# Attention and feed-forward in one pass: the products run thirteen chunks behind the attention instead of fourteen, and two row tiles share a chunk

## Chip, cores and metric

The kernel runs on one core of a Trainium2 chip. The metric is the device time of one execution in microseconds, the median of several runs. TensorE is called PE in the profile, VectorE DVE, ScalarE ACT, GpSimd POOL, and SyncE (which here only issues DMAs) SP.

## What is computed

The inputs are `x` and `ctx`, each 8 batches of 512 positions by 2048 channels.

```python
# attention by autocorrelation, d = 256 channels a head, H = 8 heads
q, k = layernorm(x), ctx                       # v = ctx as well
corr = ifft(fft(q) * conj(fft(k))).real        # along the 512 positions, each channel
w, idx = top_k(corr, 12); w = softmax(w)       # 12 lags for each channel
out = sum_i w[i] * v[min(idx[i] + pos, 511)]   # shifted values, the last one repeated
x1 = x + out
# feed-forward: one 2048 x 2048 matrix plus 16 low-rank updates, weighted
h = layernorm(x1)
y = h @ W.T + bias + sum_e coeffs[e]*scales[e] * (h @ A[e].T) @ Bf[e].T
result = x1 + y
```

## The kernel before, in words

The attention works on chunks of one batch and 256 channels: 8 chunks a batch, 64 in all. Transforms are matrix products with cosine and sine matrices on folded halves of the positions. The feed-forward folds its low-rank updates into W first, splits W and h into high and low float16 halves, and takes three of the four products of halves. A batch's feed-forward needs all 8 of its attention chunks.

**Windows.** Every engine runs one loop over windows `w`. In window `w` the attention handles chunk `w` (queries, correlation, the largest lags, weights) and the output of chunk `w - 1`. PE begins window `w` with the lag products of chunk `w - 1` (`upper_lags`, L756), and in this document a window begins there, or with its first feed-forward product when no attention is left. The feed-forward of batch `b` takes 8 windows, `8b + LAG` to `8b + LAG + 7`, in which `fill` (L878) slips 8 pieces of 12 matmuls (L848, L850, L852) between the steps of the attention. With LAG = 14 windows 0 to 13 hold attention alone, 14 to 63 both, 64 to 77 products (window 64 also has the lag products and the output of the last chunk). In windows 1 to 9 the engines also prepare W.

**Row tiles.** Between the two halves a batch passes through 4 row tiles of 128 positions by 2048 channels. Tile `r` goes this way, one tile a window in windows `8b + 9` to `8b + 12`:

- SP loads the tile of x into `rows[w % 2]`, one of two buffers (`load_rows`, L497).
- POOL issues a DMA that adds the attention's parts onto it (`add_row`, L1211).
- DVE takes its statistics (`row_statistics`, L1445 to L1450), does the attention's `part_output` (L1438, L1439), and then the inverse root and shift (`row_gain`, up to L1458).
- SP stores the tile as x1 to the output (`store_x1`, L513). When that has landed ACT normalises it (L1051) and copies the high half (L932); POOL subtracts for the low half (`row_low`, L1217) in the next window.
- SP stores both halves (`store_h`, L517 and L519). When all four tiles of a batch have landed, `load_h` (L549) turns and loads them for PE.

**Output.** Every second product window ends a group of 512 output columns. At the start of the window after it DVE multiplies the sums out of PSUM into `y`, one of two buffers (`scale_group`, L1467; L1286 in the profile), and POOL adds them onto the output with a DMA (L1238). PE may not start the next group on a PSUM bank before DVE has read it (the wait in L846).

Every engine takes its instructions in program order, and SP and POOL wait in line for the semaphore of each DMA that they issue. The attention's chain on POOL within a window is `add_products`, `add_upper`, `add_lower` (which ends in `z_added`), after which PE may run `output` (L828).

## Time and profile before

| | us |
|---|---|
| median of 3 runs (2583.07 to 2590.03) | 2583.85 |
| the profiled execution's own time | 2574.18 |
| its span, first to last instruction | 2572.4 |
| PE busy | 2438.0 (95%) |
| DVE busy | 1798.4 (70%) |
| POOL busy | 1785.6 (69%) |
| ACT busy | 1103.5 (43%) |

The profile is of one execution. It is read by stretches, since the stages have different limits: the front, windows 0 to 13, up to 496.59 us; the shared windows up to about 2250 us; the end with products alone. A wait is told with what ended it. A bracket at the end of a row gives the engine's idle time ahead of the instruction, and its releaser.

### The profile page before, as it was taken

To read this page: it belongs to the slowest core of one execution; us is meant where nothing else is said; L and a number is where in the kernel's file an instruction comes from. 1 tells how busy PE (TensorE), PEld (TensorE's weight loads), DVE (VectorE), ACT (ScalarE), POOL (GpSimd) and SP (SyncE) were. 2 spreads that over 40 slices of the span, in tenths; PEclk is the share of its full clock that TensorE was granted. 3 is DMA by queue.
4 is the path that set the end of the run, shared out by engine and by line. 5 is a ranking of instruction groups with operands and counts; after the bars stand their busy time and mean duration, and the time that the engine had idled before them with its cause. 6 is when DMAs were issued, how large, how long until landed. Compare 5 with 4: busy or idle time off the path is not lost.

```text
span 2572.4 us, 36321 instructions
## 1 busy us (share of the span) xinstructions
PE 2438.0 (95%) x12536; PEld 1529.4 (59%) x12536; DVE 1798.4 (70%) x4366; ACT 1103.5 (43%) x2166; POOL 1785.6 (69%) x1357
## 2 busy tenths in 40 slices
PE   4998966799999999999999999999999999999898
PEld 3665655566666666666666666666666666644343
DVE  5888887767887688777876788768877787731000
ACT  4787865543454344543454344444433343201000
POOL 5798988866986688876886788677886688422000
PEclk8999998899999999999999999999999999999999
DMA  9499999966999789968998799968996799689853
GB/s 336 101 262 263 273 227 243 266 200 192 285 293 237 203 245 290 262 186 246 288 281 197 196 303 291 254 174 243 284 247 172 212 294 245 134 244 311 220 138 86
DMA packets 532264, 606.03 MB, mean 236 GB/s; under 512 B 322160, under 2 KB 447216, under 8 KB 509168
## 3 DMA queue, kind: packets, MB, share of 16 engines
q1 hardware_dynamic: 505920, 503.04, 66.4%
q0 software_dynamic: 26160, 100.67, 20.2%
q8 instruction: 99, 1.62, 0.2%
q14 instruction: 85, 0.70, 0.1%
HBM read 342.53 MB, written 184.56 MB: 205 GB/s over the span
## 4 chain that ended last, share of the span: by engine, by line
PE 77%; issue 4%; DMA 3%; POOL 3%; SPq 2%; DVE 1%; ACT 0%; POOLq 0%; ACTq 0%; DVEq 0%
PE f_ps L848 16%; PE f_ps L850 16%; PE f_ps L852 16%; PE a_ps L699 10%; PE a_ps L756 5%; PE a_ps L829 3%; PE a_ps L828 3%; PE a_ps L761 2%; PE a_ps L801 2%; DMA p_lo_t<-p_lo 1%; PE a_ps L807 1%; PE a_ps L809 1%; PE a_ps L803 1%; DMA out_dram<-a_rows 1%; PE f_ps L874 1%
## 5 line engine op out<-in xcount | busy, mean ns | idle before, releaser
L848 PE MATMUL f_ps<-f_whi,f_hhi 128*128 128x512 f16 x2048 | 777.8, 380 | 15.2 <-issue 7.5
L850 PE MATMUL f_ps<-f_wlo,f_hhi 128*128 128x512 f16 x2048 | 777.7, 380 | 0.0
L852 PE MATMUL f_ps<-f_whi,f_hlo 128*128 128x512 f16 x2048 | 777.5, 380 | 0.0
L1140 POOL TENSOR_TENSOR a_zvf<-a_zvf,a_twf 128x512 f32<-128x512 f32 x256 | 337.2, 1591 | 79.3 <-DVE a_twf L1286 79.3
L852 PEld LDWEIGHTS f_ps<-f_whi,f_hlo 128*128 128x128 f16 x2048 | 200.7, 98 | 242.6 <-issue 1.9
L1140 POOL TENSOR_TENSOR a_prod<-a_prod,a_twf 128x512 f32<-128x512 f32 x64 | 81.6, 1274 | 368.5 <-DVE a_twf L1286 321.6
L848 PEld LDWEIGHTS f_ps<-f_whi,f_hhi 128*128 128x128 f16 x2048 | 200.8, 98 | 229.2 <-issue 15.3
L850 PEld LDWEIGHTS f_ps<-f_wlo,f_hhi 128*128 128x128 f16 x2048 | 200.7, 98 | 225.5 <-issue 1.4
L932 ACT ACTIVATE a_vu<-a_ps 128x512 f32<-128x512 f32 (+2 forms) x512 | 218.2, 486 | 157.4 <-PE a_ps L699 156.7
L756 PE MATMUL a_ps<-a_w_lag,lags 128*128 128x256 f16 x1536 | 231.5, 274 | 11.0 <-DVE a_twf L1286 10.4
L1286 DVE TENSOR_TENSOR a_twf<-a_ps,a_vu 128x1024 f32<-128x1024 f32 (+1 forms) x128 | 223.5, 1746 | 0.2 <-PE a_ps L699 0.2
L1286 DVE TENSOR_TENSOR f_y<-f_ps,f_scale 128x512 f32<-128x512 f32 x128 | 80.0, 682 | 198.4 <-PE f_ps L852 198.4
L932 ACT ACTIVATE a_side<-a_ps 128x1 f32<-128x1 f32 (+2 forms) x420 | 122.5, 333 | 183.4 <-PE a_ps L829 168.7
L1286 DVE TENSOR_TENSOR a_zvf<-a_ps,a_vu 128x2048 f32<-128x2048 f32 x64 | 146.5, 2290 | 55.7 <-PE a_ps L756 55.7
L756 PEld LDWEIGHTS a_ps<-a_w_lag,lags 128*128 128x128 f16 x1536 | 150.3, 98 | 54.0 <-DVE a_twf L1286 12.6
L1140 POOL TENSOR_TENSOR a_zu<-a_zu,a_zvf 128x512 f32<-128x512 f32 x128 | 179.4, 1579 | 0.0
L1140 POOL TENSOR_TENSOR a_zu<-a_zu,a_tu 128x512 f32<-128x512 f32 x128 | 165.6, 1358 | 19.2 <-DVE a_tu L1286 19.2
L1217 POOL TENSOR_TENSOR f_rowlo<-a_rows,f_rowhi 128x2048 f16<-128x2048 f32 x32 | 136.4, 4262 | 41.1 <-ACT f_rowhi L932 41.1
L1051 ACT ACTIVATE a_rows<-a_rows,f_shift,f_gain 128x2048 f32<-128x2048 f32 x32 | 67.1, 2095 | 208.1 <-DVE f_shift L1458 134.2
L1024 ACT ACTIVATE a_prod<-a_ps,a_minus_max 128x512 f32<-128x512 f32 x128 | 81.0, 684 | 165.5 <-issue 158.9
L942 ACT ACTIVATE xs<-xs,stat 128x256 f32<-128x256 f32 x256 | 132.2, 589 | 35.1 <-DVE stat L1429 31.7
L1238 POOL DMA_DIRECT2D out_dram<-f_y x31 | 48.3, 1558 | 139.4 <-DVE f_y L1286 130.1
(145 smaller groups left out, 5047.6 us busy)
## 6 DMA issues: line engine op xcount, KB each, us to landing
f_whi<-whi_scratch SPq DMA_DIRECT2D x128, 512.0 KB, 5.2
f_wlo<-wlo_scratch SPq DMA_DIRECT2D x128, 512.0 KB, 6.0
a_rows<-in_x_dram SPq DMA_DIRECT2D x62, 1024.0 KB, 9.8
vs<-in_ctx_dram SPq DMA_DIRECT2D x64, 512.0 KB, 6.2
xs<-in_x_dram SPq DMA_DIRECT2D x64, 512.0 KB, 6.0
parts_scratch<-a_so SPq DMA_DIRECT2D x64, 512.0 KB, 7.3
a_rows<-parts_scratch POOLq DMA_DIRECT2D x32, 1024.0 KB, 10.2
out_dram<-a_rows SPq DMA_DIRECT2D x32, 1024.0 KB, 11.4
```

The lines of the kernel that those rows point to most:

```text
L699: return nc.tensor.matmul(ps[:, pair, j, :], fold[:, k, :], source, start=True, stop=True)
L756: mm = nc.tensor.matmul(out, lag_mat[:, constant, 2 * cls + k, :], w_lag[:, part, main::TB, :], start=(constant + part == 0), stop=(consta ...
L828: nc.tensor.matmul(ps[:, 2 + j, i, :], outm[:, k0, :], z[:, s0, :], start=True, stop=False)
L848: nc.tensor.matmul(f_ps[:, t, :], h_hi[q][:, kq, rows_t], w_hi[u % WR][:, :, kq, :], start=(k == 0), stop=False)
L850: nc.tensor.matmul(f_ps[:, t, :], h_hi[q][:, kq, rows_t], w_lo[u % WR][:, :, kq, :], start=False, stop=False)
L852: mm = nc.tensor.matmul(f_ps[:, t, :], h_lo[q][:, kq, rows_t], w_hi[u % WR][:, :, kq, :], start=False, stop=(k == DB - 1))
L932: return nc.scalar.activation(out, source, ACT.Copy, **how)
L942: op = nc.scalar.activation(xs[n % XB][:, k, :], xs[n % XB][:, k, :], ACT.Identity, bias=gain[:, 1, k:k + 1], scale=gain[:, 0, k:k + 1])
L1024: nc.scalar.activation(wts[:, g, :], corr[:, g, :], ACT.Exp, bias=minus_max[:, g:g + 1]).then_inc(exp_done, 1)
L1140: return nc.gpsimd.tensor_tensor(whole, whole, part, op)
L1217: nc.gpsimd.tensor_tensor(row_lo[:, :], rows[w % 2][:, :], row_hi[:, :], ALU.subtract).then_inc(lo_done, 1)
L1286: return nc.vector.tensor_tensor(out, a, b, ALU.mult)
```

## The change

LAG goes from 14 to 13. For that the four row tiles of a batch are done in three windows: tile 0 in window `8b + 9`, tiles 1 and 2 in `8b + 10`, tile 3 in `8b + 11`. The buffer of a tile now goes by the tile's parity and not by the window's. The high and low halves get two buffers each, and the semaphores of the stores of x1 and of the halves are split by parity to go with them. The space comes from `y`, which has one buffer now, so that DVE may write a group only when the DMA of the group before has landed. The closing of a batch's statistics for the attention moves from window 13 to window 12 of its batch.

```diff
-LAG, KQ, WR = 14, 4, 3
+LAG, KQ, WR = 13, 4, 3
...
-        row_hi = sb("f_rowhi", [T, D], F16)
-        row_lo = sb("f_rowlo", [T, D], F16)
+        row_hi = [sb(f"f_rowhi{i}", [T, D], F16) for i in range(2)]
+        row_lo = [sb(f"f_rowlo{i}", [T, D], F16) for i in range(2)]
...
-        y = [sb(f"f_y{i}", [T, TB, WC]) for i in range(2)]
+        y = sb("f_y", [T, TB, WC])
...
+        def row_window(r):
+
+            return CHUNKS * (r // TB) + 9 + (0, 1, 1, 2)[r % TB]
+
+        def row_tiles(w):
+
+            return [r for r in range(TILES) if row_window(r) == w]
...
+            def load_row(r):
+
+                w, i = row_window(r), (r + 1) % 2
+                before = stats_before(w, i)[-1]
+                at_least(sp, rows_done, sum(stats_tile(k) is not None for k in range(before + 1)))
+                at_least(sp, lo_done, r - 1)
+                at_least(sp, pw_summed, 2 * min(w - 2, PREPARED))
+                sp.dma_start(rows[i][:, :], x_rows[r * T:(r + 1) * T, :]).then_inc(rows_in[i], 16)
...
-                if row_tile(w - 1) is not None:
-                    store_h(row_tile(w - 1))
+                for r in row_tiles(w - 1):
+                    store_h(r)
+                    if r % TB < 2:
+                        load_row(r + 2)
...
-                if r is not None:
-                    store_x1(w, r)
+                for r in row_tiles(w):
+                    if r % TB < 2:
+                        store_x1(r)
...
                 load_v(w + 3)
+                for r in row_tiles(w):
+                    if r % TB >= 2:
+                        store_x1(r)
...
-                if r is not None and r % TB > 0:
-                    add_row(w, r)
-                if row_tile(w - 1) is not None:
-                    row_low(w - 1, row_tile(w - 1))
+                for r in row_tiles(w):
+                    if r % TB == 1:
+                        add_row(r)
+                for r in row_tiles(w - 1):
+                    row_low(r)
                 if 1 <= w <= N:
                     add_upper(w - 1)
...
                 if 1 <= w <= N:
                     add_lower(w - 1)
+                for r in row_tiles(w):
+                    if r % TB >= 2 or r % TB == 0 and w < LAG:
+                        add_row(r)
...
-                at_least(dve, out_out[g % 2], 16 * (g // 2))
+                at_least(dve, out_out, 16 * g)
...
-                if r is not None:
-                    row_statistics(w, r)
+                first = [r for r in row_tiles(w) if r % TB < 2]
+                for r in first:
+                    row_statistics(r)
                 if 1 <= w <= N:
                     part_output(w - 1)
-                if r is not None:
+                for r in first:
+                    row_gain(r)
+                for r in row_tiles(w)[len(first):]:
+                    row_statistics(r)
                     row_gain(r)
```

DVE, batch 3, from the end of tile 1's root to the attention's next products (`a_prod`): before.

```order
L153 TENSOR_SCALAR f_gain<-f_sq,f_root 128x1
L1458 TENSOR_SCALAR f_shift<-f_mv,f_gain 128x1
L1286 TENSOR_TENSOR a_prod<-a_ps,a_vu 128x1024
L1286 TENSOR_TENSOR a_twf<-a_ps,a_vu 128x1024
L1286 TENSOR_TENSOR a_zu<-a_ps,a_vu 128x1024
```

The same place after the change, up to the first step of tile 2's root.

```order
L153 TENSOR_SCALAR f_gain<-f_sq,f_root 128x1
L1491 TENSOR_SCALAR f_shift<-f_mv,f_gain 128x1
L1478 BN_STATS f_bn<-a_rows 128x6 x4
L116 MEMSET a_idle 1x1
L1481 BN_AGGR f_mv<-f_bn 128x2
L1483 TENSOR_SCALAR f_veps<-f_mv 128x1
L142 TENSOR_SCALAR f_root<-f_veps 128x1
```

Tile 2's statistics and root now stand ahead of `a_prod`, and after them the four `f_y` products of `scale_group`, which before stood one window earlier and one later.

POOL, the window after tile 1's (window 35 of batch 3), from the attention's `add_products` to `z_added`: before.

```order
L1140 TENSOR_TENSOR a_prod<-a_prod,a_twf 128x512
L1184 TENSOR_TENSOR a_prod<-a_twf,a_prod 128x512
L1211 DMA a_rows<-parts_scratch 128x2048
L1217 TENSOR_TENSOR f_rowlo<-a_rows,f_rowhi 128x2048
L1140 TENSOR_TENSOR a_zu<-a_zu,a_tu 128x512 x2
L1223 DMA out_dram<-f_bias 128x2048
L1140 TENSOR_TENSOR a_zvf<-a_zvf,a_twf 128x512 x4
L1140 TENSOR_TENSOR a_zu<-a_zu,a_zvf 128x512 x2
```

The same window after the change.

```order
L1166 TENSOR_TENSOR a_prod<-a_prod,a_twf 128x512
L1210 TENSOR_TENSOR a_prod<-a_twf,a_prod 128x512
L1244 TENSOR_TENSOR f_rowlo<-a_rows,f_rowhi 128x2048 x2
L1166 TENSOR_TENSOR a_zu<-a_zu,a_tu 128x512 x2
L1251 DMA out_dram<-f_bias 128x2048 x2
L1266 DMA out_dram<-f_y 128x4x512
L1166 TENSOR_TENSOR a_zvf<-a_zvf,a_twf 128x512 x4
L1166 TENSOR_TENSOR a_zu<-a_zu,a_zvf 128x512 x2
L1238 DMA a_rows<-parts_scratch 128x2048
```

Two subtractions for low halves stand ahead of the attention's sums, and tile 3's accumulate comes behind them.

SP, last batch, from tile 0's stores of its halves (tiles 28 to 31 of the program): before.

```order
L517 DMA h_scratch<-f_rowhi 128x2048
L519 DMA h_scratch<-f_rowlo 128x2048
L497 DMA a_rows<-in_x_dram 128x2048
L513 DMA out_dram<-a_rows 128x2048
L538 DMA f_whi<-whi_scratch 128x2048
L538 DMA f_wlo<-wlo_scratch 128x2048
```

The same place after the change.

```order
L532 DMA h_scratch<-f_rowhi 128x2048
L534 DMA h_scratch<-f_rowlo 128x2048
L512 DMA a_rows<-in_x_dram 128x2048
L528 DMA out_dram<-a_rows 128x2048
L553 DMA f_whi<-whi_scratch 128x2048
L553 DMA f_wlo<-wlo_scratch 128x2048
L528 DMA out_dram<-a_rows 128x2048
L553 DMA f_whi<-whi_scratch 128x2048
L553 DMA f_wlo<-wlo_scratch 128x2048
L577 DMA f_scale<-wscale_scratch 128x512
L532 DMA h_scratch<-f_rowhi 128x2048
L534 DMA h_scratch<-f_rowlo 128x2048
```

Tile 2's store of x1 (the second L528) now stands ahead of the next weights, of the load of the scales, and of tile 1's halves, which the load of tile 3 comes behind; before it stood behind all of these.

## Rows read from the trace of the kernel before

**Rows 1.** The page, part 1: busy time of each engine.

```profile
PE 2438.0 (95%) x12536; PEld 1529.4 (59%) x12536; DVE 1798.4 (70%) x4366; ACT 1103.5 (43%) x2166; POOL 1785.6 (69%) x1357
```

**Rows 2.** Stretches: length, busy us (instructions) by engine, clock, DMA share, GB/s.

```profile
366.09:397.31 31.22, 21.98 (x114) 17.40 (x113) 26.67 (x67) 17.24 (x30) 30.41 (x21) 0.89 1.09 224
431.40:465.44 34.04, 22.11 (x114) 17.51 (x113) 26.67 (x67) 16.98 (x30) 27.91 (x22) 0.90 1.05 266
465.44:496.59 31.15, 21.74 (x105) 16.82 (x104) 24.19 (x54) 21.07 (x35) 29.08 (x23) 0.84 1.06 254
496.59:535.70 39.11, 36.93 (x189) 22.78 (x188) 26.34 (x68) 17.84 (x39) 24.12 (x20) 0.96 0.94 231
1202.17:1237.25 35.08, 35.08 (x189) 22.42 (x188) 29.31 (x75) 15.59 (x33) 30.66 (x23) 1.00 1.06 291
2277.70:2298.43 20.73, 20.73 (x98) 9.39 (x97) 6.00 (x20) 0.79 (x1) 1.79 (x2) 1.00 0.83 230
2395.01:2417.77 22.76, 22.76 (x97) 9.91 (x98) 0.00 (x0) 0.00 (x0) 0.00 (x0) 0.91 1.11 254
```

**Rows 3.** DVE in order of time, around window 34: start, length, instruction.

```profile
1200.36 2.47 DVE L1286 TENSOR_TENSOR f_y<-f_ps,f_scale 128x512 f32<-128x512 f32 x4
1202.75 1.21 DVE L1286 TENSOR_TENSOR a_prod<-a_ps,a_vu 128x1024 f32<-128x1024 f32 x1
...
1228.80 2.46 DVE L1445 BATCH_NORM_STATS2 f_bn<-a_rows 128x6 f32<-128x512 f32 x4
...
1231.67 0.69 DVE L1438 TENSOR_TENSOR a_so<-a_ps,a_side 128x512 f32<-128x512 f32 x1
...
1235.30 0.21 DVE L1458 TENSOR_SCALAR f_shift<-f_mv,f_gain 128x1 f32<-128x1 f32 x1
```

**Rows 4.** PE in order of time, window 34: second lag products, output.

```profile
1206.51 0.49 PE L756 MATMUL a_ps<-a_w_lag,lags 128*128 128x256 f16 x3
...
1226.89 0.59 PE L828 MATMUL a_ps<-a_zu,outm 128*128 128x256 f32 x2
```

**Rows 5.** POOL in order of time, window 34, from `add_products` to `z_added`.

```profile
1205.17 1.28 POOL L1140 TENSOR_TENSOR a_prod<-a_prod,a_twf 128x512 f32<-128x512 f32 x1 [9.08 <-DMA parts_scratch<-a_so]
...
1208.24 4.39 POOL L1217 TENSOR_TENSOR f_rowlo<-a_rows,f_rowhi 128x2048 f16<-128x2048 f32 x1
1212.28 2.78 POOL L1140 TENSOR_TENSOR a_zu<-a_zu,a_tu 128x512 f32<-128x512 f32 x2
...
1221.01 3.65 POOL L1140 TENSOR_TENSOR a_zu<-a_zu,a_zvf 128x512 f32<-128x512 f32 x2
```

**Rows 6.** DMA issues, 1206 to 1227 us (window 34): the last number is us to landing.

```profile
a_rows<-parts_scratch POOLq DMA_DIRECT2D x1, 1024.0 KB, 9.5
a_rows<-in_x_dram SPq DMA_DIRECT2D x1, 1024.0 KB, 10.1
```

**Rows 7.** The same, 1241 to 1250 us (window 35).

```profile
a_rows<-parts_scratch POOLq DMA_DIRECT2D x1, 1024.0 KB, 11.9
a_rows<-in_x_dram SPq DMA_DIRECT2D x1, 1024.0 KB, 16.1
```

**Rows 8.** SP in order of time, window 35 (begun at 1237.25): the load of a tile.

```profile
1247.06 0.37 SPq L497 DMA_DIRECT2D a_rows<-in_x_dram  x1
```

**Rows 9.** SP and DVE in order of time, batch 0's window 10 (366.09 to 397.31).

```profile
389.88 0.34 SPq L497 DMA_DIRECT2D a_rows<-in_x_dram  x1
...
397.90 1.22 DVE L1286 TENSOR_TENSOR a_prod<-a_ps,a_vu 128x1024 f32<-128x1024 f32 x1
```

**Rows 10.** SP, DVE and PE in order of time, the end.

```profile
2332.67 0.37 SPq L497 DMA_DIRECT2D a_rows<-in_x_dram  x1
...
2336.52 2.47 DVE L1445 BATCH_NORM_STATS2 f_bn<-a_rows 128x6 f32<-128x512 f32 x4 [24.81 <-DMA a_rows<-parts_scratch]
...
2342.90 0.38 PE L848 MATMUL f_ps<-f_whi,f_hhi 128*128 128x512 f16 x1 [2.84 <-DVE f_y L1286]
```

More of the change, by code:

```diff
@@ L426, in closed_batch, with stats_before, rows_job @@
                 return 1
-            return (w - 13) // CHUNKS + 2 if w >= 13 and (w - 13) % CHUNKS == 0 and (w - 13) // CHUNKS < BATCH - 2 else None
-        def rows_job(w):
-            return sum(stats_tile(i) is not None or row_tile(i) is not None for i in range(w % 2, w + 1, 2))
-        def row_tile(w):
-            if w >= 9 and (w - 9) % CHUNKS < 4 and (w - 9) // CHUNKS < BATCH:
-                return TB * ((w - 9) // CHUNKS) + (w - 9) % CHUNKS
-            return None
+            return (w - 12) // CHUNKS + 2 if w >= 12 and (w - 12) % CHUNKS == 0 and (w - 12) // CHUNKS < BATCH - 2 else None
+        def row_window(r):
+            return CHUNKS * (r // TB) + 9 + (0, 1, 1, 2)[r % TB]
+        def row_tiles(w):
+            return [r for r in range(TILES) if row_window(r) == w]
+        def stats_before(w, parity):
+            return [i for i in range(w) if i % 2 == parity and stats_tile(i) is not None]
+        def rows_job(w, parity):
+            return len(stats_before(w + 1, parity)) + sum(row_window(r) <= w and (r + 1) % 2 == parity for r in range(TILES))
         def product_window(w):
@@ L486, in load_v, with load_stats @@
                 shared.load_v(sp, n)
-            def load_rows(w):
-                m, r = stats_tile(w), row_tile(w)
-                if m is None and r is None:
+            def load_stats(w):
+                m = stats_tile(w)
+                if m is None:
                     return
                 at_least(sp, rows_done, sum(stats_tile(i) is not None for i in range(w - 1)))
-                at_least(sp, lo_done, sum(row_tile(i) is not None for i in range(w - 1)))
+                at_least(sp, lo_done, max([r + 1 for r in range(TILES) if (r + 1) % 2 == w % 2 and row_window(r) < w],
+                                          default=0))
                 at_least(sp, pw_summed, 2 * min(w - 2, PREPARED))
-                source = r if m is None else m + TB
-                sp.dma_start(rows[w % 2][:, :], x_rows[source * T:(source + 1) * T, :]).then_inc(rows_in[w % 2], 16)
+                sp.dma_start(rows[w % 2][:, :], x_rows[(m + TB) * T:(m + TB + 1) * T, :]).then_inc(rows_in[w % 2], 16)
+            def load_row(r):
[5 more added lines that the diff above has]
+                sp.dma_start(rows[i][:, :], x_rows[r * T:(r + 1) * T, :]).then_inc(rows_in[i], 16)
             def store_parts(n):
@@ L630, in _ @@
                 if 0 < w <= PREPARED:
-                    load_rows(w + 1)
+                    load_stats(w + 1)
+                    for r in row_tiles(w + 1):
+                        load_row(r)
                 load_x(w + 3)
@@ L1045, in copy_output, with row_normalise, row_high @@
                 copy(skew[:, :, :], ps[:, 2:4, 1, :]).then_inc(out_copied, 1)
-            def row_normalise(w, r):
+            def row_normalise(r):
+                row = rows[(r + 1) % 2]
                 act.wait_ge(f_shift_done, r + 1)
-                act.wait_ge(x1_out, 16 * (r + 1))
-                nc.scalar.activation(rows[w % 2][:, :], rows[w % 2][:, :], ACT.Identity, bias=f_shift[:, 0:1],
-                                     scale=f_gain[:, 0:1]).then_inc(h_done, 1)
-            def row_high(w, r):
+                act.wait_ge(x1_out[r % 2], 16 * (r // 2 + 1))
+                nc.scalar.activation(row[:, :], row[:, :], ACT.Identity, bias=f_shift[:, 0:1], scale=f_gain[:, 0:1]
+                                     ).then_inc(h_done, 1)
+            def row_high(r):
                 act.wait_ge(h_done, r + 1)
-                at_least(act, h_out, 32 * r)
-                copy(row_hi[:, :], rows[w % 2][:, :]).then_inc(hi_done, 1)
+                at_least(act, h_out[r % 2], 32 * (r // 2))
+                copy(row_hi[r % 2][:, :], rows[(r + 1) % 2][:, :]).then_inc(hi_done, 1)
             def tile_sums(w, n):
@@ L1273, in _ @@
                     add_lower(w - 1)
+                for r in row_tiles(w):
+                    if r % TB >= 2 or r % TB == 0 and w < LAG:
+                        add_row(r)
                 if w == PREPARED + 2:
```

93 lines of the change are left out of this document (48 added, 45 removed).

## The prediction, made before the changed kernel ran

> **What bounds the kernel now.** I read the busy times first: PE is busy 95% of the span, the next engine 70% [rows 1]. That average hides three stages, so I cut the span at the windows [rows 2]. Window 34, in the shared stage, takes 35.08 us with PE busy all of it: the bound is PE alone. A window with attention alone takes 31 to 34 us with PE busy 22: there the bound is the chain through POOL, DVE and ACT, with the DMA engines full (share above 1). A window with products alone takes 20.73 us. Next come the instructions around window 34, for how much time each engine has in hand before PE must wait [rows 3 to 8], and last the front [rows 9] and the end [rows 10].
>
> What the smaller LAG is worth: one attention window becomes shared, one window of products alone goes. Windows 13 and 14 took 31.15 + 39.11 us (the 39.11 holds the wait for the first products); as two shared windows they take 39.11 + 35.08, so +3.9. The window that goes was worth 20.7, but the end of the kernel must be able to use it. From the start of window 65 (2277.70) to the first product of the last batch (2395.01) there were 117.3 us, and PE's own work in them was 5 x 20.7 = 103.6. The rest was waiting for the row tiles.
>
> **The shared stage: batches 1 to 6, six double windows.** I take window 34 (start 1202.17) with tiles 1 and 2 of its batch, and write +x for us after a window's start.
>
> DVE. Tile 1's statistics start at 1228.80, +26.6, and its shift ends at 1235.51, +33.3, the attention's two outputs (1.2) among them. A tile alone is 2.87 (1228.80 to 1231.67) plus 6.71 - 2.87 - 1.2 = 2.6, so 5.5 [rows 3]. Tile 2 behind it ends at +38.8, 3.8 into window 35. By the new parity the four `f_y` stand next, 2.4 (1200.36 to 1202.75), then the attention's two products, 2.4: done at +8.5 of window 35. PE wants them before its second lag products at +4.34 (1206.51 - 1202.17) [rows 4]. In window 35 PE waits 4.2, part of it already on the first product of the new group, which needs `f_y`.
>
> POOL. It starts `add_products` when DVE's products are done, at +8.5 in place of +3.0, and needed 19.5 to the end of `z_added` (1205.17 to 1224.66) [rows 5]. Now two low halves stand in that stretch: 4.04 more (1208.24 to 1212.28). The issue of a second bias DMA comes in and the issue of an accumulate goes out, which cancels. So `z_added` is at 8.5 + 19.5 + 4.0 = +32.1, where PE wanted to start the output at +24.7 (1226.89) [rows 4]. PE's whole wait in window 35 is 7.4, DVE's 4.2 inside it.
>
> Tile 2's data. Its load is issued where tile 3's was, at about +9.8 [rows 8], lands 10.1 [rows 6] or 16.1 [rows 7] later, POOL issues the accumulate right behind (it is there at about +20), and that lands 9.5 or 11.9 later: +29.4 to +37.8. DVE wants it at +33.3. So 0 to 4.5 more; I take 1.8, a little below the middle, since the group's DMA has left window 34.
>
> Tile 3. POOL issues its accumulate behind `z_added`, at +32.1 of window 35; it lands at +41.6 to +44. DVE's 5.5 follow, and 2.4 of products: +49.5 to +51.9. Window 36 starts at 35.08 + 7.4 = 42.5 and wants the products 4.34 later, at +46.8: 2.7 to 5.1 of wait. I take 3.0. Behind DVE in line stand the attention's next chunk, and behind POOL's accumulate the folds for the next chunks; they have a window in hand.
>
> Sum: 7.4 + 1.8 + 3.0 = 12.2 a batch, 73 for six. Nothing gives it back, since PE had no idle time in these windows. Bounds: 4.2 (DVE alone counts) to 7.4 + 4.5 + 5.1 = 17, so 25 to 102.
>
> The Trainium skill ("DMA: Bandwidth & Descriptors", Issuing engines are not separate DMA queues) says that DMAs started by SP and by GpSimd run on the same 16 engines and only interleave. By that rule two tiles in one window find no second path, and each should land like the slower row; by that the 1.8 would be 4.5, and the total 16 more. The trace agrees so far as the same load took 10.1 in one window and 16.1 in the next [rows 6, 7].
>
> **The front (batch 0).** Tile 2's load goes out at 389.88 [rows 9], lands about 10 later at 400, the accumulate (up to 11.9 here) at about 412, and DVE needs 5.5: 417.4, where the attention's next products began at 397.90 [rows 9]. That is 19.5, with POOL's folds held up behind the accumulate too. Tile 3 does the like one window on; from the shared stage I take 5. Window 12 loses its tile, and a window without the stall of one is 3 shorter (34.04 against 31.15) [rows 2]. 19.5 + 5 - 3 = 21.5. Bounds 5 (the landings are hidden) and 30.
>
> **The end.** In window 66 DVE now waits for tile 2's accumulate, which landed at 2336.5 [rows 10], 58.8 after window 65 began; its load still hangs on tile 0. `f_y` of the group finished in window 66 stands behind that and 5.5 of statistics, so PE begins window 67 at about +65, and is through window 68 at 65 + 2 x 20.7 = +106, +108.5 if it restarts as slowly as window 70 did (22.76 against 20.73) [rows 2]. Before, the same wait stood a window later and cost 2.84 [rows 10]. SP also holds tile 1's halves and tile 3's load behind tile 2's store and the load of the scales: the load goes out at about +65.5, where it was at +55.0 (2332.67) [rows 10]. If everything from that load to the first product takes its old 62.3 us, the last batch starts at +127.8. With fewer weights loaded meanwhile it will be less. Between 108.5 and 127.8 I take 118, which is +1 to the 117.3. The window saved is not seen here. Bounds: -34 (PE alone, 4 x 20.7 = 83) and +11.
>
> **Sum.** 3.9 + 73 + 21.5 + 1 = +99. The one buffer of `y` costs nothing in it: a group's DMA has two windows, 70 us, to land. On the profiled execution: its span 2572.4, its own time 2574.18, so 2673 us. The median of the runs shown lies 9.7 above that execution, so I give 2583.85 + 99 = 2683.
>
> **Rivals.**
> - It fits, and the end shortens (faster). DVE is only 29.3 of 35.08 busy in window 34 [rows 2], room for 5.5 by the sum. If the shared and front windows hold their time and the last batch starts when PE is free, 3.9 - 34.4 = -30: 2553. Against it: the room lies ahead of +26.6, where DVE waits in its chain, and the last tile's path runs through four landings one after another. 0.07.
> - The two cancel: 25 + 3.9 + 5 - 34: 2584. It needs the end at PE's limit, against the 58.8 us of tile 2. 0.04.
> - DVE's overflow alone: POOL's low halves find room. 25 + 3.9 + 5 to 12: 2618 to 2625. Against it, the 19.5 that I read. 0.11.
> - The clock. In the windows where PE waits, the granted clock drops from 2.4 to 1.2 GHz for a while, as ahead of window 70 (clock 0.91, 2.0 us lost) [rows 2]. Twelve such windows at 2.0: +24, 2707. Against it: these waits are shorter than the 13.7 us of waiting ahead of window 70, and lie between full stretches. 0.15.
>
> The Trainium skill ("TensorE: Matmul & The Clock Gate", Why this matters for your kernels) warns that idle gaps between bursts of matmuls send the clock back to half rate. By it the clock is likelier to drop on the longer waits than on those of 2 to 4 us. The row of window 70 agrees for the waits ahead of it.
>
> **How the numbers follow.** My own case has 0.63. All but the first two rivals are slower. Range: low 2630 (7.4 x 6 = 44, LAG 3.9, front 5, end -8), high 2725 (six at 16 is 96, 3.9, 30, 11); what lies below and above is 2 in 10. A measurement tells about 0.3%, 8 us, from no change: faster 0.07, same 0.04, slower 0.89.
>
> **What would show it.** Right: in the window after each double one PE waits on `f_y` and on the lag products' release, then at L828's output for POOL's `a_zu`, some 7 us together; that window is about 42.5 us and the one behind it 38; twelve longer windows and the rest at 35.08. In the front DVE waits for the accumulate in window 10. In the end PE stands some 23 us ahead of window 67. Wrong: those windows at 35.08, or the last batch starting 83 to 100 us after window 65. I am most in doubt about tile 3 and the last chain.

## The result, and the profile of the changed kernel

The changed kernel takes 2752.26 us, the median of 4 runs (2744.47 to 2764.84); the kernel before, beside it, 2583.46 (4 runs, 2576.97 to 2590.03). The ratio is 1.0658, 95% interval 1.063 to 1.0686: slower. The direction had been forecast, the size not: +99 us forecast, +169 measured. The profiled execution took 2744.47, its span is 2742.7, so 170.3 more than the span of before.

Busy times on the page of the changed kernel:

```profile
PE 2469.0 (90%) x12516; PEld 1536.9 (56%) x12516; DVE 1821.9 (66%) x4372; ACT 1098.2 (40%) x2168; POOL 1789.3 (65%) x1359
```

PE does the same matmuls as in [rows 1] (some records are missing) and is busy 31.0 us longer for them. Next the stretches, as in [rows 2] (length, busy us of PE, PEld, DVE, ACT and POOL, granted clock, DMA share, GB/s): windows 9, 11, 12, then 34, 35, 36, then from window 65 to the last batch's first product, and the window behind it.

```profile
330.62:374.05 43.43, 21.48 (x114) 16.77 (x112) 27.77 (x72) 20.35 (x34) 28.58 (x20) 0.79 0.93 201
405.59:459.05 53.46, 24.06 (x113) 19.02 (x112) 27.41 (x69) 21.21 (x32) 44.98 (x31) 0.71 0.96 233
459.05:501.47 42.42, 22.34 (x105) 17.52 (x104) 28.78 (x71) 18.29 (x34) 28.94 (x23) 0.80 0.88 223
1282.77:1317.85 35.08, 35.08 (x190) 22.43 (x189) 29.37 (x76) 15.47 (x33) 29.80 (x23) 1.00 1.02 276
1317.85:1366.91 49.06, 35.81 (x190) 22.11 (x188) 30.11 (x77) 17.78 (x34) 36.05 (x26) 0.99 1.03 259
1366.91:1406.79 39.88, 38.15 (x189) 23.38 (x189) 33.25 (x83) 17.05 (x36) 28.44 (x21) 0.93 0.95 262
2433.52:2563.42 129.90, 86.04 (x386) 38.10 (x384) 26.36 (x82) 16.01 (x8) 27.15 (x15) 0.83 0.91 248
2563.42:2586.03 22.61, 22.61 (x97) 9.83 (x98) 0.00 (x0) 0.00 (x0) 0.00 (x0) 0.91 1.09 284
```

Against before, whose windows 9, 11 and 12 took 35.28, 34.09 and 34.04, the 170.3 split as follows. "A window like 35" is the one at that place in its batch: 19, 27, 35, 43, 51 and 59.

- Windows 9 to 12: +36.2.
- Windows 13 and 14, where LAG acts: +4.3.
- Windows 15 to 64: +115.5, 113.5 of it in three windows a batch: those like 35 average 48.8 (47.6 to 51.4), like 36 39.3, like 37 36.1. The others stay within about 1 us of 35.08.
- The end: +12.6 (129.9 against 117.3), and behind it +1.9, the last window.

Window 35 on PE, only the rows with a wait (start, length, instruction, in brackets the wait ahead of it and what ended it):

```profile
1322.39 0.38 PE L874 MATMUL f_ps<-f_whi,f_hhi 128*128 128x512 f16 x1 [2.64 <-DVE f_y L1319]
...
1326.36 0.50 PE L782 MATMUL a_ps<-a_w_lag,lags 128*128 128x256 f16 x3 [1.22 <-DVE a_twf L1319]
...
1349.96 0.67 PE L854 MATMUL a_ps<-a_zu,outm 128*128 128x256 f32 x2 [3.05 <-POOL a_zu L1166]
...
1366.91 0.82 PE L782 MATMUL a_ps<-a_w_lag,lags 128*128 128x256 f16 x3 [6.34 <-DMA a_w_lag<-a_w_row]
```

The first three sum to 6.9, where 7.4 was forecast. The last is new: window 36 cannot begin, since the transposed lag weights have not landed. SP turns these weights with two transposing DMAs, called the lag transposes below, and in the shared stage every window begins with the products that use them. Here is SP's row of their issue:

```profile
1348.01 14.00 SPq L523 DMA_TRANSPOSE a_w_lag<-a_w_row  x2
```

The DMAs issued from 1338 to 1350 (last number: median us to landing):

```profile
out_dram<-f_bias POOLq DMA_DIRECT2D x2, 1024.0 KB, 11.0
out_dram<-f_y POOLq DMA_DIRECT2D x1, 1024.0 KB, 20.2
a_rows<-parts_scratch POOLq DMA_DIRECT2D x1, 1024.0 KB, 16.9
a_w_lag<-a_w_row SPq DMA_TRANSPOSE x2, 17.4
```

In the kernel before, window 34, where a group's DMA was still in flight, had for the same pair:

```profile
a_w_lag<-a_w_row SPq DMA_TRANSPOSE x2, 6.1
```

and windows 32 and 40, with nothing of GpSimd's in flight, 3.1 and 3.2 us. SP is held by the issue too, for 14 us, with weights, the store of x1 and the parts behind it. On DVE and ACT tile 3 is then late in window 36:

```profile
1365.53 2.47 DVE L1478 BATCH_NORM_STATS2 f_bn<-a_rows 128x6 f32<-128x512 f32 x4 [9.92 <-DMA a_rows<-parts_scratch]
```

```profile
1375.46 2.09 ACT L1078 ACTIVATE a_rows<-a_rows,f_shift,f_gain 128x2048 f32<-128x2048 f32 x1 [21.17 <-DMA out_dram<-a_rows]
```

PE's rows of all six batches add the 113.5 us up, to within rounding: 37.0 are waits for DVE and POOL inside the windows like 35 (the three rows above), 31.4 are waits for the lag transposes at their end (3.5 to 6.9 each), 7.4 are waits for the next lag transposes at the end of the windows like 36, 5.7 are other short waits in windows like 36 and 37, and 32.2 are busy time that PE has more for the same products. Some 26 of the 32.2 are the clock, an estimate: in 13 stretches of windows 15 to 63, 61.4 us in all, it was granted at its lower level (1.2 GHz), PE was busy for 51.9 us of them, and half of that is lost.

### The profile page after: what moved, and what is told of

The parts are those of the page before. It is cut to its first block and busy times, and to the rows that moved or that the text cites. A ratio compares the mean times of both kernels' runs of the same rounds, so it can differ in the third digit from the quotient of the medians.

```text
span 2742.7 us, 36295 instructions
## 1 busy us (share of the span) xinstructions
PE 2469.0 (90%) x12516; PEld 1536.9 (56%) x12516; DVE 1821.9 (66%) x4372; ACT 1098.2 (40%) x2168; POOL 1789.3 (65%) x1359
## 5 line engine op out<-in xcount | busy, mean ns | idle before, releaser
L1166 POOL TENSOR_TENSOR a_zvf<-a_zvf,a_twf 128x512 f32<-128x512 f32 x256 | 330.0, 1478 | 92.7 <-DVE a_twf L1319 92.7
L782 PE MATMUL a_ps<-a_w_lag,lags 128*128 128x256 f16 x1536 | 243.2, 284 | 84.6 <-DVE a_twf L1319 43.7
L782 PEld LDWEIGHTS a_ps<-a_w_lag,lags 128*128 128x128 f16 x1536 | 153.3, 101 | 137.9 <-DVE a_twf L1319 51.4
L1078 ACT ACTIVATE a_rows<-a_rows,f_shift,f_gain 128x2048 f32<-128x2048 f32 x32 | 67.1, 2096 | 351.3 <-DMA out_dram<-a_rows 221.9
L958 ACT ACTIVATE a_side<-a_ps 128x512 f32<-128x512 f32 (+1 forms) x422 | 122.2, 330 | 202.5 <-PE a_ps L855 185.4
L1478 DVE BATCH_NORM_STATS2 f_bn<-a_rows 128x6 f32<-128x512 f32 x128 | 78.9, 680 | 163.2 <-DMA a_rows<-parts_scratch 163.2
L1166 POOL TENSOR_TENSOR a_zu<-a_zu,a_tu 128x512 f32<-128x512 f32 x128 | 162.2, 1305 | 19.5 <-DVE a_tu L1319 19.5
L1166 POOL TENSOR_TENSOR a_zu<-a_zu,a_zvf 128x512 f32<-128x512 f32 x128 | 172.3, 1469 | 0.0
L958 ACT ACTIVATE a_tu<-last 1x256 f32<-1x256 f32 x64 | 26.2, 410 | 321.4 <-DVE a_tu L1319 321.4
```

The source lines that it names most:

```text
L782: mm = nc.tensor.matmul(out, lag_mat[:, constant, 2 * cls + k, :], w_lag[:, part, main::TB, :], start=(constant + part == 0), stop=(consta ...
L958: return nc.scalar.activation(out, source, ACT.Copy, **how)
L1078: nc.scalar.activation(row[:, :], row[:, :], ACT.Identity, bias=f_shift[:, 0:1], scale=f_gain[:, 0:1]).then_inc(h_done, 1)
L1166: return nc.gpsimd.tensor_tensor(whole, whole, part, op)
L1478: op = nc.vector.bn_stats(f_bn[:, j, :], rows[(r + 1) % 2][:, j * WC:(j + 1) * WC])
```

## Experiments

First the change was taken apart from its far end. Each kernel of this ladder differs from the next by one group of edits; all times are medians, the ratio is to the kernel before, timed on the same chip. The last columns are from the traces: windows 9 to 14, 15 to 64, and window 65 to the last batch's first product. A trace is of one execution, and two of these lie well off their median: that of e2 took 15.5 less, that of e1 13.9 more. So a step of the last columns need not equal the step of the medians.

```
kernel                                     us       ratio (95%)              9-14   15-64    end
before                                     2583.5   1                        204.9  1742.1   117.3
own halves, one y, DVE's order (g2)        2597.9   1.0062 (1.0033, 1.0091)  219.3  1749.6   117.7
+ closing, scales a window earlier (g1)    2638.3   1.0217 (1.0184, 1.0250)  225.9  1784.8   117.4
+ SP stores x1 of tiles 2, 3 later (f1)    2661.1   1.0303 (1.0270, 1.0335)  233.4  1784.6   129.0
+ POOL's later accumulates (e2)            2704.9   1.0465 (1.0429, 1.0500)  230.1  1803.5   143.5
+ tiles 1 and 2 share a window (e1)        2783.8   1.0764 (1.0729, 1.0800)  239.7  1900.3   142.6
+ LAG 13: the changed kernel               2752.3   1.0658 (1.0630, 1.0686)  245.4  1857.5   129.9
```

**Single tiles, LAG 14 (e2).**

```
-LAG, KQ, WR = 13, 4, 3
+LAG, KQ, WR = 14, 4, 3
-            return CHUNKS * (r // TB) + 9 + (0, 1, 1, 2)[r % TB]
+            return CHUNKS * (r // TB) + 9 + (0, 1, 2, 3)[r % TB]
```

> The changed kernel with LAG 14 and one row tile a window again, at windows 9, 10, 11, 12. What is left of the change: own halves for even and odd tiles, one y, the places of the later tiles' accumulates and of tile 0's in batch 0, the statistics' closing one window earlier. My theory says that these cost next to nothing but in batch 0 (tile 0's accumulate moved behind the lower sums: window 9 is 8 longer than before): 2592, with window 34 to 36 at 35.08. Rival (the later place of the accumulates of tiles 2 and 3 costs in each batch, 2 to 3 us each): 2610 to 2620.

2704.88 us. Both theories fell short: with no shared window and the old LAG 122 us stay. Windows 36 and 37, and the end:

```profile
1326.95:1364.51 37.56, 35.65 (x189) 22.18 (x188) 27.98 (x66) 15.23 (x32) 29.85 (x23) 1.00 0.95 260
1364.51:1406.79 42.28, 37.71 (x188) 23.41 (x189) 31.95 (x90) 21.25 (x41) 29.36 (x22) 0.92 0.97 266
2363.86:2507.32 143.46, 105.39 (x482) 47.05 (x481) 27.99 (x84) 16.02 (x8) 27.22 (x15) 0.88 0.89 240
```

At the end tile 31's x landed at 2425.14, but POOL issues the accumulate behind tile 30's low half:

```profile
2447.78 4.06 POOL L1244 TENSOR_TENSOR f_rowlo<-a_rows,f_rowhi 128x2048 f16<-128x2048 f32 x1 [27.43 <-ACT f_rowhi L958]
2451.79 0.86 POOL L1251 DMA_DIRECT2D out_dram<-f_bias  x1
2452.39 1.59 POOL L1266 DMA_DIRECT2D out_dram<-f_y  x1
2453.14 1.78 POOL L1238 DMA_DIRECT2D a_rows<-parts_scratch  x1
```

**The same, POOL's accumulates in their old places (f1).**

```
                 for r in row_tiles(w):
-                    if r % TB == 1:
+                    if r % TB > 0:
                         add_row(r)
...
-                    if r % TB == 0 and w >= LAG:
+                    if r % TB == 0:
...
-                for r in row_tiles(w):
-                    if r % TB >= 2 or r % TB == 0 and w < LAG:
-                        add_row(r)
```

> The kernel with single tiles and LAG 14 (1.0465 of before), and in it alone the accumulates on POOL back where they were before the change: tiles 1 to 3 right behind the attention's products, tile 0 ahead of the bias. New theory (POOL's late place of the accumulates is what cost the 120 us there: 59 in the shared windows, 25 in the front, 26 at the end, where tile 31's accumulate went out 28 us after its data had landed): all of it goes, 2590, with the windows at 35.08 and the last batch 117 us after window 65. Rival (own halves, one y or SP's later store of x1 carry part of it): 2620 to 2660; the one y would show as DVE waiting for the group's DMA, the store of x1 as ACT waiting for it.

2661.08: 44 of the 122 go, not all. The two traces differ by 29.9 only, 14.5 of it at the end and 19 in the shared windows. The rival named a part of the rest rightly: tile 3's accumulate landed at 1337.9, SP stored its x1 16.7 us later, behind the lag transposes, and ACT waited:

```profile
1354.52 0.74 SPq L528 DMA_DIRECT2D out_dram<-a_rows  x1
```

```profile
1362.84 2.09 ACT L1078 ACTIVATE a_rows<-a_rows,f_shift,f_gain 128x2048 f32<-128x2048 f32 x1 [12.84 <-DMA out_dram<-a_rows]
```

**And SP's stores of x1 in their old place (g1).**

```
                 for r in row_tiles(w):
-                    if r % TB < 2:
-                        store_x1(r)
+                    store_x1(r)
...
-                for r in row_tiles(w):
-                    if r % TB >= 2:
-                        store_x1(r)
```

> The kernel with single tiles, LAG 14 and POOL's old places (1.0303 of before), and in it SP's stores of x1 back where they were, ahead of the lag transposes. Theory (in the profiled run tile 3's accumulate landed at 1337.9 and its x1 store went out at 1354.5, so ACT stood 12.8 us for it and everything behind it in window 37 was late): ACT's wait goes, window 37 from some 40 to 36, the end 129 to 119, in the front 10 us: 2661 - 6 x 4 - 10 - 10 = 2617. Rival (the closing of the statistics one window earlier, 3.0 us on DVE ahead of window 37's products, makes window 37): only the end and the front gain, 2640.

2638.26, 23 less: the rival's total. The end gave 11.6 back (129.0 to 117.4), and window 37 went from 40.7 to 36.8 as the theory had it, but windows 22, 30 and 38 are 4.5 to 9.2 longer than 35.08 in this kernel, so windows 15 to 64 sum to the same. Windows 9, 36, 37 and the end:

```profile
333.52:376.39 42.87, 22.82 (x113) 18.12 (x112) 25.70 (x68) 17.98 (x32) 25.12 (x19) 0.79 0.95 198
1323.33:1359.55 36.22, 35.25 (x190) 22.33 (x188) 30.47 (x77) 15.59 (x32) 30.42 (x23) 1.00 1.04 274
1359.55:1396.34 36.79, 35.25 (x189) 22.37 (x188) 29.29 (x78) 21.48 (x41) 28.66 (x22) 1.00 0.98 256
2344.09:2461.49 117.40, 105.78 (x481) 47.19 (x480) 28.01 (x84) 16.01 (x8) 27.12 (x15) 0.97 1.01 288
```

**And the closing of the statistics and the stores of the scales in their old windows (g2).**

```
-            return (w - 12) // CHUNKS + 2 if w >= 12 and (w - 12) % CHUNKS == 0 and (w - 12) // CHUNKS < BATCH - 2 else None
+            return (w - 13) // CHUNKS + 2 if w >= 13 and (w - 13) % CHUNKS == 0 and (w - 13) // CHUNKS < BATCH - 2 else None
...
-                if PREPARED <= w < PREPARED + TB:
-                    for n in range(TB * (w - PREPARED), TB * (w - PREPARED + 1)):
+                if PREPARED + 1 <= w < PREPARED + 1 + TB:
+                    for n in range(TB * (w - PREPARED - 1), TB * (w - PREPARED)):
```

> As the kernel before it, and the closing of the statistics and the stores of the weights' scales back in their old windows. What is left of the change: own halves for even and odd tiles, one y, the later tiles' statistics behind the attention's output on DVE, the places of x loads. Theory (those cost nothing): 2580 to 2590, window 9 at 35 again (the scale stores stood ahead of the store of the parts, for which tile 0's accumulate waits). Rival (one y or own halves cost): above 2600, with DVE waiting for the group's DMA.

2597.87, 40 less. Windows 9, 36 and the end:

```profile
329.96:363.64 33.68, 20.95 (x114) 16.71 (x113) 26.18 (x69) 19.15 (x33) 24.87 (x18) 0.90 0.97 264
...
1288.30:1324.77 36.47, 35.42 (x190) 22.28 (x188) 30.68 (x78) 15.59 (x32) 30.64 (x23) 1.00 1.05 271
2298.77:2416.49 117.72, 105.96 (x482) 47.14 (x481) 28.00 (x84) 16.01 (x8) 27.12 (x15) 0.97 1.01 287
```

Window 9 gives 9.2 back, which settles it: the scale stores stood ahead of the store of the attention's parts, for which tile 0's accumulate waits. The parts land 5.0 us after their issue here, 10.4 in the changed kernel, and POOL issues the accumulate 0.6 behind the landing in both. Windows like 37 give 1.7 each back (the closing is some 3 us of DVE ahead of the next products). Windows 22, 30 and 38 are at 35.08 again; in g1 PE waited there for lag transposes (9.1 us ahead of window 23). SP issued them at +34.5, +34.2 and +30.6 of the window, where +26.0 is usual, and they took 8.9 to 9.8 us with nothing of GpSimd's in flight. Why was not settled. What is left, 16 us, a little above the theory, was not taken apart further. In the traces it lies in the windows like 36 (1.1 to 1.9 each, 7.9 in all, where PE waits 0.96 for DVE's products, and the later tiles' statistics now stand behind the attention's output on DVE) and in the front, 14.4. The front's windows scatter: f3 below, with the front of the kernel before, has 210.2 in place of 204.9. No wait of DVE for a group's DMA shows.

**Shared window, LAG 14 (e1).**

```
-LAG, KQ, WR = 13, 4, 3
+LAG, KQ, WR = 14, 4, 3
```

> The changed kernel with LAG back at 14; the shared window of two row tiles, own halves and one y stay. The groups finish in even windows again, so no f_y stands ahead of the attention's products in window 35 and no group's DMA in it. My theory (the group's DMA stretches the lag transposes): window 35 is 40 us, with 1.8 of wait for DVE inside 4.9 for POOL, and the transposes land in 3 to 7 us; window 36 is 37 to 38. Sum against before: 6 x (5 + 2.5) + 8 for the front, and the end 5 to 14 shorter, since tile 31 comes a window earlier ahead of an unmoved window 70: 2625. Rival (tile 3's accumulate stretches the transposes): they still take 15 to 18 us, window 35 is 45 to 46, the time 2655.

2783.8, well above both. Windows like 34 take 41.2 now and windows like 35 50.1. The groups finish in even windows again, so their DMA stands in GpSimd's queue ahead of tile 2's accumulate, and the first lag transpose of the windows like 34 lands in 13.5 to 15.4 us; in those like 35 in 11 to 26 beside tile 3's accumulate, with no group's DMA there. So both theories had a piece: whatever of GpSimd's is in flight counts. By the medians LAG 13 gains 1% against this kernel.

**What holds the lag transposes.** Five kernels, all from the changed one; only the added lines are shown. In e3 the group's DMA is cut to 16 of 128 partitions, which leaves seven eighths of that group out of the output. In e4 tile 3's accumulate is cut the same way:

```
+                part = T // 8 if g % 4 == 2 else T
+                nc.gpsimd.dma_start(out[b, :, cols].rearrange("(i p) d -> p i d", p=T)[0:part], y[0:part, :, :],
```

```
+                part = T // 8 if r % TB == 3 and r >= TB else T
+                nc.gpsimd.dma_start(rows[i][0:part, :], part_rows[r * T:r * T + part, :], accum_op=ALU.add
```

> The changed kernel, with the group's DMA to out in windows 19, 27, 35 and so on (the third group of a batch) cut to 16 of 128 partitions, so seven eighths of that group's products are left out of the output. My theory (that DMA stretches the lag transposes behind it): in window 35 the transposes land in 3 to 8 us in place of 17.9, the wait of 6.3 before the upper lags goes to under 1, and window 35 is 42 to 43 in place of 49.1; time 2752 - 7 x 6 = 2710. Rival (tile 3's accumulate does it): transposes stay at 15 to 18, window 35 at 48 to 49.

> The changed kernel, with the accumulate of the attention's parts onto tile 3 of batches 1 to 7 cut to 16 of 128 partitions (the other rows of that tile lack the attention's output). My theory (the group's DMA stretches the transposes, tile 3's accumulate only adds to it): transposes at 12 to 16 us, window 35 at 46 to 48; window 36, which waits for DVE behind this accumulate, 2 to 3 shorter than its 39.9. Rival (tile 3's accumulate stretches them): transposes in 3 to 8, window 35 at 42 to 43.

Tile 3's accumulate behind the transposes (f4), as a plain load, which leaves x out of that tile (f5), and ahead of the group's DMA (f6, where it is then skipped at its old place):

```
+                        if r % TB == 3 and LAG <= w < N:
+                            pool.wait_ge(w_dma, 32 * dma_turns(w + 1))
                         add_row(r)
```

```
+                how = {} if r % TB == 3 and r >= TB else dict(accum_op=ALU.add)
```

```
                 for r in row_tiles(w - 1):
                     add_bias(r)
+                for r in row_tiles(w):
+                    if r % TB == 3 and LAG <= w < N:
+                        add_row(r)
                 if g is not None:
                     add_group(g)
```

> The changed kernel, with POOL waiting for the lag transposes to land before it issues tile 3's accumulate (batches 1 to 6). The time at which that accumulate landed (47.6 into window 35) is about where it would land anyway from an issue at 37 to 38. Theory (an accumulate of the parts and the lag transposes in flight together hold each other up): the transposes land in 6.5 to 11 us (the group's DMA stays beside them), the last wait of window 35 goes from 6.3 to under 1.5, and window 35 from 49 to 43; window 36 stays within 1.5 of 39.9. Time 2752 - 6 x 6 = 2716. Rival (bias and group DMAs do it, or the number of DMAs in flight): transposes stay at 15 to 18.

> The changed kernel, with tile 3's accumulate (batches 1 to 7) as a plain load of the same bytes from the same queue, without the addition (that tile then holds the attention's output without x). If the addition is what holds the transposes up: they land in 6 to 11 us, window 35 at 43. If it is any DMA of GpSimd's queue, or its place behind the group's DMA in that queue: 15 to 18, window 35 at 48 to 49. I lean to the second, 0.6.

> The changed kernel, with tile 3's accumulate (batches 1 to 6) on POOL ahead of the group's DMA and of the attention's lower sums, at about +23 of window 35, where its load has just landed (in the profiled run 1340.85, POOL comes by at 1340.5). Theory (overlap with the transposes, and the late place): it lands at +34 to +36, only 4 us into the transposes, which take 6 to 11; window 35 43 to 44; DVE has tile 3 in time, so window 36 36 to 37 in place of 39.9. Time 2752 - 6 x 9 = 2698. Rival (transposes wait for whatever GpSimd's queue holds when they are issued, now the group's DMA behind the accumulate, landing at +44): transposes at 15, window 35 at 46 to 48, only window 36 gains, 2725.

Window 35 of each, in us from the issue of the first transpose; "mean" is over the six windows of that place:

```
                       group's DMA  accumulate  transposes    mean 35  mean 36   time us
changed kernel            12.7         17.5     17.9, 18.8      48.8     39.3    2752.3
small group's DMA (e3)     9.4         31.6     31.5, 32.6      50.3     39.7    2749.4
small accumulate (e4)     12.0         13.4     13.9, 14.7      44.7     39.3    2716.5
accumulate later (f4)     11.7          -       12.2, 13.1      43.9     49.8    2774.2
plain load (f5)           12.1         14.7     15.1, 16.0      45.9     39.7    2729.1
accumulate first (f6)     15.5          9.6     16.0, 16.9      47.6     39.5    2745.4
before, window 34          5.6          -        6.5,  7.4
before, window 32           -           -        3.2,  4.4
```

In every row with a DMA of GpSimd's the second transpose lands 1 to 2 us behind the last of them that was issued before it, whether it adds or only loads, large or small. The traces of all 18 kernels say the same of every window: where such a DMA, issued before the second transpose, landed over 8 us after the issue of the first (88 pairs), the second transpose landed 0.2 to 1.9 us behind it. It is not the only thing that counts: of 678 pairs with none in flight half took 4.4 to 4.5 us, but some up to 9.8. Whether the transposes wait their turn or share the same engines no run tells.

The row of e3 is its longest window: the six range from 44.1 to 62.8, with accumulates that took 12.5 to 31.2 us, and why they differ so much is open. My first theory, that the group's DMA alone does it, fell with e3. The second, overlap with the accumulate, is a part of it: f4 shortens window 35 by 4.9, but the group's DMA still holds the transposes for 12. And f4 is slower in sum, since tile 3 then stands 10 us later in window 36: DVE's products stand behind it, and PE waits 13.75 us for them. f6 lands the accumulate early and puts the group's DMA last, and the transposes wait for that one, as its rival said. Windows 35 and 36 of f4:

```profile
1327.73:1371.06 43.33, 35.81 (x190) 22.09 (x188) 28.72 (x74) 17.80 (x34) 23.46 (x15) 1.00 0.97 267
1371.06:1421.38 50.32, 36.57 (x188) 23.03 (x189) 32.65 (x89) 17.45 (x36) 40.58 (x31) 0.86 0.93 239
```

**The second low half later (e5).** `row_low(2)` behind `add_lower`, `store_h(2)` behind the transposes.

> The changed kernel, with the low half of each second tile (of batches 1 to 7) made on POOL behind the attention's lower sums in place of ahead of the upper, and its halves stored behind the lag transposes on SP. My theory (POOL's wait before the output, 3.05, is the two low halves in a row, 4.0): that wait goes from 3.05 to 1 or less, and what is gained is kept only if the transposes do not then end the window: they land when they land, so window 35 goes from 49.1 to 47 to 49. Rival (the wait is DVE's delay handed on): the 3.05 stays within 0.5.

The wait for `a_zu` is gone from window 35, so the two low halves make that term. But the time is 2829.55: three of the six windows took 58.9 to 78.3, with the transposes beside an accumulate, h stores and weights. Why all of these land so late is open. Of the DMAs issued from 1985 to 1988:

```profile
a_rows<-parts_scratch POOLq DMA_DIRECT2D x1, 1024.0 KB, 48.2
a_w_lag<-a_w_row SPq DMA_TRANSPOSE x2, 37.5
```

These two were issued in window 51, ahead of whose end PE waited 39.8.

**Tile 0's place in the front (e6).** Both conditions on `w` and LAG at `add_row` taken out, so tile 0 is always ahead of the bias.

> The changed kernel, with tile 0's accumulate of batch 0 ahead of the lower sums on POOL as it was before. My theory (its later place cost window 9 its 8.15): window 9 goes from 43.4 back to 35 to 36, the time 8 less, if window 10 and 11 do not give it back. Rival (window 9's wait comes of tile 1's load or the second DMA in that window): window 9 stays at 42 to 44.

2756.91, window 9 at 41.8 and window 10 at 37.9: the theory fell. SP's order in window 9 shows the cause, first in the kernel before, then in the changed one: four stores of the scales stand ahead of the parts.

```profile
341.54 0.51 SPq L501 DMA_DIRECT2D parts_scratch<-a_so  x1
...
343.26 4.56 SPq L578 DMA_TRANSPOSE p_hi_t<-p_hi  x1
347.92 0.53 SPq L497 DMA_DIRECT2D a_rows<-in_x_dram  x1
```

```profile
341.60 2.48 SPq L713 DMA_DIRECT2D wscale_scratch<-p_down  x4
344.13 0.43 SPq L516 DMA_DIRECT2D parts_scratch<-a_so  x1
...
345.21 10.35 SPq L594 DMA_TRANSPOSE p_hi_t<-p_hi  x1
355.66 0.53 SPq L512 DMA_DIRECT2D a_rows<-in_x_dram  x1
```

**The end: order around tile 30 (e7), tile 31's accumulate first (g3).** e7 puts tile 30's statistics behind window 67's `f_y` on DVE and its x1 store into window 67. g3:

```
                 for r in row_tiles(w - 1):
                     row_low(r)
+                    if r == TILES - 3:
+                        add_row(TILES - 1)
...
```

Its old place is left out, and SP stores this tile's x1 ahead of the weights.

> The changed kernel, but at the end alone tile 30's statistics and gain stand behind window 67's f_y on DVE, and its store of x1 on SP stands in window 67 ahead of the stores of h. My theory (PE stood 18.1 us for f_y behind the statistics of tile 30): the wait ahead of window 67 goes from 18.1 to under 3, and the first product of the last batch comes 5 to 12 us sooner after window 65 began (129.9 now), since part of the time is then waited for tile 31. Rival (tile 31's own chain sets that start, 62 us from its load): it stays at 128 to 130, and only the place of the waiting changes.

> The changed kernel, and at the end alone tile 31's accumulate on POOL ahead of tile 30's low half and so of two biases and the group's DMA, its x1 store ahead of the last weight loads of its window. In the profiled run it went out at 2506.35 behind them and took 24.7 us to land, as long as the group's DMA ahead of it in GpSimd's queue. Theory (an accumulate lands behind what stands ahead of it in that queue): it lands 10 to 15 us after its issue, the last batch starts 10 to 14 us sooner, 129.9 to 117 to 120: 2740. Rival (the DMA engines are simply full there): it still takes 22 to 25 us, 2750.

e7: 2753.09 us. PE no longer stands ahead of window 67, and the last batch starts 132.3 after window 65: its rival was right, the wait only moved. g3: 118.8 in place of 129.9, as expected; 2742.76 us, ratio 1.0625 (1.0589 to 1.066). POOL in the changed kernel and in g3:

```profile
2496.65 4.06 POOL L1244 TENSOR_TENSOR f_rowlo<-a_rows,f_rowhi 128x2048 f16<-128x2048 f32 x1 [9.33 <-ACT f_rowhi L958]
2500.65 1.76 POOL L1251 DMA_DIRECT2D out_dram<-f_bias  x2
2501.78 1.95 POOL L1266 DMA_DIRECT2D out_dram<-f_y  x1
2506.35 0.91 POOL L1238 DMA_DIRECT2D a_rows<-parts_scratch  x1 [2.62 <-DMA a_rows<-in_x_dram]
```

```profile
2509.09 0.88 POOL L1238 DMA_DIRECT2D a_rows<-parts_scratch  x1 [19.80 <-DMA a_rows<-in_x_dram]
```

The first accumulate landed 24.7 us after its issue. The second was issued at +73.7 of window 65 in place of +72.8, but with nothing ahead of it, and landed in 7.9.

**Two tries at a faster kernel.** e9 is e2 with `(0, 1, 1, 2)` for the last batch alone; f3 is the kernel before, with tile 29's load in window 64 and its accumulate right behind tile 28's.

> As the kernel before in LAG (14) and in batches 0 to 6 (one row tile a window), but in the last batch alone tiles 29 and 30 share window 66, so tile 31 is done in window 67. My theory: the interior windows are as before, the last batch's first product comes 7 to 14 us sooner (tile 31's load no longer waits a window), the front gives 8 back by tile 0's place in batch 0: 2580, that is 10 below the kernel with single tiles everywhere. Rival (the chain through DVE and the transposes of h is as long with the tiles doubled, as the changed kernel's end was 12.6 longer with a window less of PE work ahead): no gain or 5 worse, 2590 to 2597.

> The kernel before with one change at the end: the load of tile 29 goes out in window 64 beside that of tile 28, and its accumulate right behind tile 28's. Tile 29's accumulate lands at about 2298 in place of 2306 in the profiled run; its statistics stand behind f_y of window 66 on DVE, so the chain to tile 31 gains 5 us. PE has 13.7 us of waiting ahead of the last batch. My theory: 5 to 8 us faster, 2576. Rival (two accumulates at once land later, and the chain through tile 31's load is stretched by the same DMA engines): within 3 us of before.

e9: 2695.36, ratio 1.0437 (1.0411 to 1.0464); its base, e2, is at 1.0465 (1.0429 to 1.05), and the end is 142.4 against 143.5 in the traces, so no gain is shown. It carried e2's misplaced accumulates. f3: 2578.9, ratio 0.9992 (0.9974 to 1.001): the end shrank from 117.3 to 115.3 in its trace, no gain that can be measured. No kernel here beats the one before.

## Why the prediction was right in sign and 70 us short

The forecast was 71 us under the 170.3: 42.5 of it in windows 15 to 64, 14.7 in the front, 11.6 at the end, 2 in the last window.

- LAG itself, +3.9: measured 4.3. Right, though window 13 alone takes 36.4 to 41.9 us in the kernels with LAG 13.
- DVE's overflow in window 35, 4.2, inside 7.4 with POOL: measured 3.9 inside 6.9. Right, and e5 confirms the low halves in it. Over the six batches it is 37.0, where 44.4 was forecast.
- Tile 2's data, 1.8 (bounds 0 to 4.5): 0 in batch 3. It landed at 1314.57, +31.8 of window 34, where DVE wanted it at +33.3.
- Tile 3, 3.0 a batch: windows like 36 are 4.2 over 35.08, but that is luck. PE waited 0.5 us or less for DVE's products there, 1.0 in all six. Window 35 had become 49 long in place of 42.5, so tile 3's statistics, done at 1371.17, pushed DVE's products only to +4.3 of window 36 (+0.6 in window 34 of the kernel before). Of the 25.3 us in six windows 15.8 are PE's greater busy time, most of it at the lower clock, and 7.4 the wait for the next lag transposes.
- "PE's whole wait in window 35 is 7.4": this step failed. I followed DVE and POOL, but not SP's lag transposes, which end the window. The second of them landed 17 to 21 us after the first was issued, beside the group's DMA and tile 3's accumulate, both of which the change puts into window 35. PE waited 3.5 to 6.9 us for them in each of six windows, 31.4 us. The rule of the Trainium skill that I cited ("DMA: Bandwidth & Descriptors", Issuing engines are not separate DMA queues) would have pointed there, had I put it to every DMA of the window and not to tile 2's alone. The traces go further than it: these landings follow GpSimd's last DMA within 2 us.
- The clock stood among the rivals, at 24 us, and was put at nothing in the sum. It belongs there: in window 36 PE is busy 38.15 for the work that takes 35.08, at a mean clock of 0.93, behind a wait of 6.3 us. In the 18 windows like 35, 36 and 37 PE is busy 32.2 us more, some 26 of it by the clock: about what the rival said.
- Front, 21.5: measured 36.2. The 19.5 for tile 2's accumulate was right (window 11 is 19.4 longer, and PE waits 18.8 for DVE's products). Missed: the scale stores, which the change moves a window earlier, ahead of SP's store of the parts (the list of the change does not name them), 8 to 9 us in window 9 (g2); and window 12, +8.4 where I had 2.
- End, +1: measured +12.6. Tile 31's load went out at +62.8 (forecast +65.5) but needed 67.1 from there where I had expected less than the old 62.3, since its accumulate lands behind three DMAs of its own queue; with it first the term is +1.5 (g3).
- One `y` at no cost: held, within the 2 us by which the last window is longer.
- Named in no step: SP's later stores of x1, the earlier closing, and POOL's later accumulates away from the shared window. In the kernel without shared windows they cost 23, a part of 40, and 44 us. What the shared windows would cost without them was not tried, so the 169 is not a sum of separate prices.

So sharing and overflow against the smaller LAG were not the whole question: the kernel with neither already takes 122 us more than the one before.

## What to carry to other kernels

Of a moved step, list every engine's queue that it passes, DMA queues included, and follow the transfer that ends the window, not only the engines. A transfer with a deadline should not be issued while long DMAs of GpSimd's queue are in flight, and an urgent one goes first in that queue. Where a change bundles a few "free" reorderings with its main idea, price or time these first: here they cost 107 us by themselves, with one row tile a window and the old LAG.

## What the runs showed of the hardware that was not expected

- The second of SP's two transposing DMAs lands within 2 us behind the last DMA of GpSimd's queue that is ahead of it. In us from the issue of the first: 4.4 alone, 7.4 behind one that landed at 5.6, 13 to 19 behind others, 49 at worst (e5). SP's own issue is held meanwhile (14.00 us for a pair, 5.41 in window 34 of the kernel before, 2.62 in window 32).
- DMAs of GpSimd's queue landed in the order of issue in all 1764 neighbouring pairs of the 18 traces: a 1 MB accumulate took 7.9 us alone in it, 24.7 behind two biases and a group's DMA; cut to an eighth it still landed 1.4 us behind the one ahead of it.
- Four stores of 512 bytes each, one number a partition, took 10.0 to 10.9 us to land (f1, window 9), and the 512 KB store of the parts behind them 11.5, in place of 5.0 in the kernel before.
- Around waits of 2 to 7 us in the shared stage the granted clock was at its lower level (1.2 GHz) 13 times, for 3.4 to 10.2 us, some 2 us lost each time. At the end it was low for 20.5 and 27.3 us, which began inside waits of 18.1 and 25.7 us and went on 5.8 and 3.9 us behind them.
